# Attention and feed-forward block on eight cores: the projection groups of the next head are spread singly between the score matmuls instead of in pairs behind them

## The chip, the cores and the metric

The kernel runs on all eight cores of one Trainium2 chip. No core talks to another: each takes one half of the 2048 query rows of one of the four batch entries, and computes K and V for all 2048 rows of that entry itself. The metric is the device time of the slowest core in microseconds (us). The program before was run eight times: median 2807.35 us, lowest 2803.17, highest 3047.69. Six of the eight lie between 2803.17 and 2808.51 us, the other two at 2934.46 and 3047.69.

## The reference

```python
def attn(x, w_q, w_k, w_v, w_o):            # 16 heads of 128, D = 2048, S = 2048, B = 4
    q = (x @ w_q.T).reshape(B, S, H, Hd)    # k and v alike
    scores = einsum('bqhd,bkhd->bhqk', q, k) / sqrt(128)
    p = softmax(scores, axis=-1)
    o = einsum('bhqk,bkhd->bqhd', p, v).reshape(B, S, D)
    return o @ w_o.T
def ffn(x, w_gate, w_up, w_down):           # hidden 8192
    return (silu(x @ w_gate.T) * (x @ w_up.T)) @ w_down.T
x = x + layernorm(attn(layernorm(x), ...))
x = x + layernorm(ffn(layernorm(x), ...))
```

## The kernel before, in words

The kernel is written engine by engine: every operation is appended to the list of its engine in the order in which the Python text emits it, and each engine works through its own list in that order. Waits are explicit: an engine stops at a wait until a counter that another engine raises has reached a number. So the order of the text is the order of the work on each engine, and an instruction that waits holds back all that stands behind it on that engine.

The stages are: layer norm and transpose of the input; the query projection of all heads (L307); the attention stage; the output projection (L565) with the two layer norms around it; the gate and up projections (L653, L665); the down projection (L712); and the last layer norm with the residual. Only the attention stage is touched.

**The attention stage** loops over 16 heads. In this text a head has four rounds, r = 0 to 3, and each round handles four tiles of 128 keys:

- *Scores* S0 to S15 (`emit_scores_tc`, L426): two matmuls of 128x512 for a tile of 128 keys by 1024 queries, into one of two PSUM areas of two banks each, used in turn.
- *Exponentials* E0 to E15 (L435) on ScalarE: read one score area, write one of four slots of the tile PTR. E(n) of a round waits for its scores, for the value product of the round before (L448, counter tRd), because that product reads PTR, and for the sum of the round before on VectorE (counter vSm), which reads PTR too. S(n) waits for E(n-2), which frees the score area.
- *Value product* PV0 to PV3 (`emit_pv_round`, L448): eight matmuls that read the four PTR slots of one round. It is emitted one round late: PV(r-1) stands behind the first two score tiles of round r.
- *Sum* (`emit_tree_round`, L459 to L477): four VectorE additions per round for the softmax denominator.
- *Filler* (`emit_kv_group`, L354): the K and V projections of the **next** head, in eight groups K0 to K3 and V0 to V3 of 16 matmuls each, two groups per round. Each is accumulated in PSUM bank 4 or 5 and copied out by ScalarE (`emit_kv_evac`, L371). A group waits until the group two before it has been copied out. K0 and K1 wait also for the reciprocal of the head before (L525, counter vRc), since the reciprocal reads banks 4 and 5.

Behind the last round stand PV3, the transposes of V for the next head (L386, copied to SBUF by VectorE at L398), two matmuls with ones that sum the denominator over partitions (L517), then on VectorE the reciprocal (L525, its input in banks 4 and 5) and the scaling of the output (L529). The first two score tiles of a head wait for the two copies at L398. The last head has no next one and no filler.

The names used below: S, E, PV, K and V with a number as above; "evacuation" is the ScalarE copy at L371; "round 0" begins at S0.

Of the kernel before, what the change touches and what calls it, by code (L numbers as in the profile page):

```python
# [13 lines left out]
H = 16  # L14
# [63 lines left out]
def build_nc():  # L78
# [23 lines left out]
    def Bv(off, dims, parts=128):  # L102
        return bass.AP(ABF, off, [[ABF_N, parts]] + [list(d) for d in dims])

    def Fv(off, dims, parts=128):
        return bass.AP(AFP, off, [[AF32_N, parts]] + [list(d) for d in dims])

    def Pv(off, dims, parts=128):
        return bass.AP(PS, off, [[4096, parts]] + [list(d) for d in dims])
# [58 lines left out]
    def op(e, f, ride=None):  # L168
        pair = None
        if ride is not None:  # L170
            c, k = ride
            c.n += k
            pair = (c.s, k)
        if pair is None:
            ops[e].append(f)
        else:
            def g(eng, f=f, pair=pair):
                f(eng).then_inc(*pair)
            ops[e].append(g)

    def w(e, c, v=None):
        if v is None:
            c, v = c
        ops[e].append(lambda eng, s=c.s, v=v: eng.wait_ge(s, v))
# [149 lines left out]
    def emit_kv_group(kind, h, g):  # L334
        slot, dwv = wk_slot[h] if kind == "K" else wv_slot[h]
        if g == 0:
            w("t", dW[slot], dwv)
        if kind == "K":
            if h == 0:
                w("t", vA, 4 * (g + 1))  # L340
            if h == 0 and g < 2:
                w("t", sQe, 16)
            elif g < 2 and h >= 1:
                w("t", kv_evac[("V", h - 1, g + 2)])
            elif g >= 2:
                w("t", kv_evac[("K", h, g - 2)])
            if h >= 2 and g < 2:
                w("t", vRc, h - 1)
        else:
            w("t", kv_evac[("K", h, g + 2)] if g < 2 else kv_evac[("V", h, g - 2)])  # L350
        bank = 4 + (g % 2)
        for kc in range(NKC):
            ride = (tKV, 1) if kc == NKC - 1 else None
            op("t", lambda e, slot=slot, kc=kc, g=g, bank=bank: e.matmul(  # L354
                Pv(bank * 512, [(1, 512)]),
                Bv(W3 + slot * 2048 + kc * 128, [(1, 128)]),
                Bv(LN1 + kc * 2048 + g * 512, [(1, 512)]),
                start=(kc == 0), stop=(kc == NKC - 1)), ride)
        kv_mm[(kind, h, g)] = (tKV, tKV.n)
        if kind == "K" and g == 3:  # L360
            consumed_at[16 + 2 * h] = (tKV, tKV.n)
        if kind == "V" and g == 3:
            consumed_at[17 + 2 * h] = (tKV, tKV.n)

    def emit_kv_evac(kind, h, g):
        w("s", kv_mm[(kind, h, g)])
        if kind == "V" and g == 0 and h >= 1:
            w("s", vt_mm[(h - 1, 1)])
        bank = 4 + (g % 2)
        dst = (KSB + (h % 2) * 2048) if kind == "K" else VFM  # L370
        op("s", lambda e, g=g, dst=dst, bank=bank: e.activation(  # L371
            Bv(dst + g * 512, [(1, 512)]),
            Pv(bank * 512, [(1, 512)]), AF.Copy), (sKV, 1))
        kv_evac[(kind, h, g)] = (sKV, sKV.n)
# [38 lines left out]
    for h in range(H):  # L413

        def emit_scores_tc(tc, h=h):
            pair = tc % 2
            if tc == 0:
                w("t", kv_evac[("K", h, 3)])
                w("t", vVt, 2 * h + 1)
            elif tc == 1:  # L420
                w("t", vVt, 2 * h + 2)
            else:
                w("t", sE, 16 * h + tc - 1)
            for half in range(2):
                ride = (tS, 1) if half == 1 else None
                op("t", lambda e, tc=tc, half=half, pair=pair, h=h: e.matmul(  # L426
                    Pv(pair * 1024 + half * 512, [(1, 512)]),
                    Bv(KSB + (h % 2) * 2048 + tc * 128, [(1, 128)]),
                    Bv(QF + h * 1024 + half * 512, [(1, 512)]),
                    start=True, stop=True), ride)  # L430
            r = tc // 4
            w("s", tS, 16 * h + tc + 1)
            w("s", tRd, 4 * h + r)
            w("s", vsm, 4 * h + r)
            op("s", lambda e, tc=tc, pair=pair: e.activation(  # L435
                Bv(PTR + (tc % 4) * 1024, [(1, 1024)]),
                Pv(pair * 1024, [(1, 1024)]),
                AF.Exp, bias=Fv(ST + 41, [(1, 1)]), scale=QK), (sE, 1))

        def emit_pv_round(r, h=h):  # L440
            w("t", sE, 16 * h + 4 * (r + 1))
            if r == 0:
                w("t", vO, h)
            for i in range(4):
                tcv = 4 * r + i
                for half in range(2):
                    ride = (tRd, 1) if (i == 3 and half == 1) else None
                    op("t", lambda e, tcv=tcv, i=i, half=half, r=r: e.matmul(  # L448
                        Pv(3072 + half * 512, [(1, 512)]),
                        Bv(VTM + tcv * 128, [(1, 128)]),  # L450
                        Bv(PTR + i * 1024 + half * 512, [(1, 512)]),
                        start=(r == 0 and i == 0), stop=(r == 3 and i == 3)), ride)

        def emit_tree_round(r, h=h):
            w("v", sE, 16 * h + 4 * (r + 1))
            with_lp = "bf16 softmax denominator tree (rvr impact <1e-5)"
            def t1f(e):
                with nc.allow_low_precision(with_lp):
                    return e.tensor_tensor(Bv(WDA, [(1, 1024)]),  # L459
                                           Bv(PTR, [(1, 1024)]),  # L460
                                           Bv(PTR + 1024, [(1, 1024)]), ALU.add)
            def t2f(e):
                with nc.allow_low_precision(with_lp):
                    return e.tensor_tensor(Bv(WDA + 1024, [(1, 1024)]),
                                           Bv(PTR + 2048, [(1, 1024)]),
                                           Bv(PTR + 3072, [(1, 1024)]), ALU.add)
            def t3f(e):
                with nc.allow_low_precision(with_lp):
                    return e.tensor_tensor(Bv(WDA, [(1, 1024)]),
                                           Bv(WDA, [(1, 1024)]),  # L470
                                           Bv(WDA + 1024, [(1, 1024)]), ALU.add)
            def accf(e, r=r):
                with nc.allow_low_precision(with_lp):
                    if r == 0:
                        return e.tensor_copy(Bv(RB, [(1, 1024)]),
                                             Bv(WDA, [(1, 1024)]))
                    return e.tensor_tensor(Bv(RB, [(1, 1024)]),  # L477
                                           Bv(RB, [(1, 1024)]),
                                           Bv(WDA, [(1, 1024)]), ALU.add)
            op("v", t1f, (vI, 1))  # L480
            op("v", t2f, (vI, 1))
            w("v", vI, vI.n)
            op("v", t3f, (vI, 1))
            w("v", vI, vI.n)
            op("v", accf, (vsm, 1))

        for r in range(4):
            emit_scores_tc(4 * r)
            emit_scores_tc(4 * r + 1)
            if r >= 1:  # L490
                emit_pv_round(r - 1)
            emit_scores_tc(4 * r + 2)
            emit_scores_tc(4 * r + 3)
            if h + 1 < H:
                if r < 2:
                    emit_kv_group("K", h + 1, 2 * r)
                    emit_kv_evac("K", h + 1, 2 * r)
                    emit_kv_group("K", h + 1, 2 * r + 1)
                    emit_kv_evac("K", h + 1, 2 * r + 1)
                else:  # L500
                    emit_kv_group("V", h + 1, 2 * (r - 2))
                    emit_kv_evac("V", h + 1, 2 * (r - 2))
                    emit_kv_group("V", h + 1, 2 * (r - 2) + 1)
                    emit_kv_evac("V", h + 1, 2 * (r - 2) + 1)
            emit_tree_round(r)
        emit_pv_round(3)
        if h + 2 < H:
# [426 lines left out]
```

How the kernel before makes its waits and increments, by code:

```python
            def g(eng, f=f, pair=pair):  # L177
                f(eng).then_inc(*pair)
# [2 lines left out]
    def w(e, c, v=None):  # L181
        if v is None:
            c, v = c
        ops[e].append(lambda eng, s=c.s, v=v: eng.wait_ge(s, v))
```

## Time and profile before

| | before |
|---|---|
| median of 8 runs | 2807.35 us (2803.17 to 3047.69) |
| time of the profiled execution | 2803.17 us |
| its span, slowest core (core 1) | 2801.6 us |
| spans of the eight cores | 2790.1 to 2801.6 us |
| TensorE matmul busy | 2393.0 us, 85% |
| VectorE busy | 647.8 us, 23% |
| ScalarE busy | 590.1 us, 21% |
| L354, K and V projection | 513.5 us in 2048 matmuls |
| L426 / L448, scores / value product | 148.6 / 124.1 us in 512 matmuls each |
| L525, reciprocal | 104.8 us in 16 |

The span is the time between the first and the last instruction of one core; the time of an execution has 1.57 us more. "Idle before" is time in which the engine stood still just ahead of a group, with the instruction that ended most of it. The granted clock (PEclk) is the share of the full TensorE rate that the chip allowed in a stretch.

### The profile page before, as it was taken

The page shows a single profiled execution, that of the slowest core. Times are in us where ns is not written, and L with a number is a line of the kernel's source. Part 1 is how long each engine was busy: PE and PEld are TensorE (multiplying, and loading weights), DVE is VectorE, ACT ScalarE, POOL GpSimd, SP SyncE. Part 2 cuts the span into 40 slices and gives each one's busy share as a digit, 9 for nine tenths or more (in the row PEclk, how much of TensorE's full clock was granted, in tenths as well). Part 3 has the DMA queues.
Part 4 walks back from the last instruction along what each step waited for, and adds up shares of the span by engine and source line. Part 5 has one row for each costly group of instructions (what it writes and reads, how often), then busy time and mean ns, then how long its engine had stood idle before and what let it go on. Part 6 is the DMA issues. An engine that isn't in the chain of part 4 may idle for free.

```text
span 2801.6 us, 26992 instructions; the slowest of 8 cores (2790.1 to 2801.6 us)
## 1 busy us (share of the span) xinstructions
PE 2393.0 (85%) x10912; PEld 1059.9 (38%) x10912; DVE 647.8 (23%) x760; ACT 590.1 (21%) x677; POOL 157.7 (6%) x269
## 2 busy tenths in 40 slices
PE   1998788888788888687799999999999999999960
PEld 1443333333333333233444444444444444444420
DVE  5501433333433333465400100000000001010021
ACT  5513333333333333222000000000000001010021
POOL 0000000000000000000000000000000000111000
PEclk9999989998998998888899999999999999999985
DMA  6541100100100100723444444444444445545478
GB/s 189 137 89 23 23 16 15 23 16 15 23 16 16 23 15 1 120 90 105 76 75 76 75 77 78 78 77 76 75 76 76 82 61 75 75 69 77 73 123 155
DMA packets 67624, 186.35 MB, mean 67 GB/s; under 512 B 4912, under 2 KB 37680, under 8 KB 62256
## 3 DMA queue, kind: packets, MB, share of 16 engines
q0 software_dynamic: 64048, 159.47, 34.3%
q1 hardware_dynamic: 3456, 25.17, 3.0%
q8 instruction: 89, 1.46, 0.2%
q14 instruction: 31, 0.25, 0.0%
HBM read 302.12 MB, written 25.17 MB: 117 GB/s over the span
## 4 chain that ended last, share of the span: by engine, by line
PE 77%; DVE 9%; DMA 4%; issue 4%; ACT 3%; another core or an unknown queue 2%; ACTq 0%; DVEq 0%; POOL 0%; POOLq 0%
PE ps L354 18%; PE ps L653 16%; PE ps L665 16%; PE ps L712 15%; PE ps L307 4%; PE ps L448 4%; DVE afp L525 4%; PE ps L426 3%; ACT abf L435 2%; DMA x2s<-afp 2%; DVE afp L194 1%; DMA out<-afp 1%; DVE abf L398 1%; DVE afp L582 1%
## 5 line engine op out<-in xcount | busy, mean ns | idle before, releaser
L354 PE MATMUL ps<-abf 128*128 128x512 bf16 x2048 | 513.5, 415 | 54.7 <-DVE afp L525 53.4
L712 PE MATMUL ps<-abf 128*128 128x512 bf16 x2048 | 448.3, 382 | 16.0 <-DVE abf L736 8.6
L653 PE MATMUL ps<-abf 128*128 128x512 bf16 x2048 | 454.2, 380 | 2.6 <-DVE abf L633 2.6
L665 PE MATMUL ps<-abf 128*128 128x512 bf16 x2048 | 452.5, 379 | 0.0
L354 PEld LDWEIGHTS ps<-abf 128*128 128x128 bf16 x2048 | 214.9, 105 | 348.6 <-issue 147.9
L435 ACT ACTIVATE abf<-ps,afp 128x1024 bf16<-128x1024 f32 x256 | 270.5, 1111 | 166.8 <-PE ps L448 103.6
L712 PEld LDWEIGHTS ps<-abf 128*128 128x128 bf16 x2048 | 200.8, 98 | 263.5 <-issue 27.5
L653 PEld LDWEIGHTS ps<-abf 128*128 128x128 bf16 x2048 | 200.6, 98 | 245.6 <-issue 5.0
L665 PEld LDWEIGHTS ps<-abf 128*128 128x128 bf16 x2048 | 200.6, 98 | 241.4
L681 DVE TENSOR_TENSOR abf<-afp,ps 128x1024 bf16<-128x1024 f32 x64 | 78.2, 1222 | 809.2 <-PE ps L665 809.2
L426 PE MATMUL ps<-abf 128*128 128x512 bf16 x512 | 148.6, 386 | 124.9 <-ACT abf L435 105.8
L676 ACT ACTIVATE afp<-ps 128x1024 f32<-128x1024 f32 x64 | 65.5, 1023 | 804.4 <-PE ps L653 804.4
L371 ACT ACTIVATE abf<-ps 128x512 bf16<-128x512 f32 x128 | 76.4, 597 | 444.9 <-PE ps L354 444.9
L459 DVE TENSOR_TENSOR abf<-abf 128x1024 bf16<-128x1024 bf16 x64 | 44.1, 690 | 516.0 <-ACT abf L435 516.0
L565 PE MATMUL ps<-abf 128*128 128x512 bf16 x512 | 126.9, 415 | 31.7 <-DVE abf L605 23.4
L448 PE MATMUL ps<-abf 128*128 128x512 bf16 x512 | 124.1, 386 | 4.6 <-DVE abf L529 3.1
L426 PEld LDWEIGHTS ps<-abf 128*128 128x128 bf16 x512 | 38.9, 96 | 223.5 <-issue 202.3
L307 PE MATMUL ps<-abf 128*128 128x512 bf16 x512 | 114.9, 386 | 2.7 <-DVE abf L266 2.7
L736 DVE CAST abf<-ps 128x512 bf16<-128x512 f32 x16 | 9.9, 684 | 438.2 <-PE ps L712 438.2
L525 DVE RECIPROCAL afp<-ps 128x1024 f32<-128x1024 f32 x16 | 104.8, 6549 | 1.3 <-PE ps L517 1.3
L719 ACT ACTIVATE abf<-ps 128x512 bf16<-128x512 f32 x16 | 8.3, 604 | 444.3 <-PE ps L712 444.3
L565 PEld LDWEIGHTS ps<-abf 128*128 128x128 bf16 x512 | 53.2, 105 | 105.8 <-issue 55.8
(78 smaller groups left out, 976.6 us busy)
## 6 DMA issues: line engine op xcount, KB each, us to landing
abf<-wg POOLq DMA_DIRECT2D x64, 512.0 KB, 5.1
abf<-wu POOLq DMA_DIRECT2D x64, 512.0 KB, 5.1
abf<-wd POOLq DMA_DIRECT2D x64, 512.0 KB, 5.4
afp<-xb SPq DMA_DIRECT2D x24, 1024.0 KB, 7.1
abf<-wq POOLq DMA_DIRECT2D x16, 512.0 KB, 7.9
abf<-wk POOLq DMA_DIRECT2D x16, 512.0 KB, 5.2
abf<-wv POOLq DMA_DIRECT2D x16, 512.0 KB, 5.1
abf<-wo POOLq DMA_DIRECT2D x4, 2048.0 KB, 34.5
```

What stands on the lines that cost most here:

```text
L307: op("t", lambda e, slot=slot, kc=kc, half=half, pair=pair: e.matmul(Pv(2048 + pair * 1024 + half * 512, [(1, 512)]), Bv(W3 + slot * 2048 ...
L354: op("t", lambda e, slot=slot, kc=kc, g=g, bank=bank: e.matmul(Pv(bank * 512, [(1, 512)]), Bv(W3 + slot * 2048 + kc * 128, [(1, 128)]), Bv ...
L371: op("s", lambda e, g=g, dst=dst, bank=bank: e.activation(Bv(dst + g * 512, [(1, 512)]), Pv(bank * 512, [(1, 512)]), AF.Copy), (sKV, 1))
L426: op("t", lambda e, tc=tc, half=half, pair=pair, h=h: e.matmul(Pv(pair * 1024 + half * 512, [(1, 512)]), Bv(KSB + (h % 2) * 2048 + tc * 12 ...
L435: op("s", lambda e, tc=tc, pair=pair: e.activation(Bv(PTR + (tc % 4) * 1024, [(1, 1024)]), Pv(pair * 1024, [(1, 1024)]), AF.Exp, bias=Fv(S ...
L448: op("t", lambda e, tcv=tcv, i=i, half=half, r=r: e.matmul(Pv(3072 + half * 512, [(1, 512)]), Bv(VTM + tcv * 128, [(1, 128)]), Bv(PTR + i ...
L525: op("v", lambda e: e.reciprocal(Fv(T1, [(1, 1024)]), Pv(2048, [(1, 1024)])), (vRc, 1))
L565: op("t", lambda e, kc=kc, j=j, qc=qc, pair=pair: e.matmul(Pv(pair * 2048 + j * 512, [(1, 512)]), Bv(OFM + kc * 1024 + qc * 128, [(1, 128) ...
L653: op("t", lambda e, slot=slot_g, kc=kc, half=half, gb=gb: e.matmul(Pv(gb * 512 + half * 512, [(1, 512)]), Bv(W3 + slot * 2048 + kc * 128, ...
L665: op("t", lambda e, slot=slot_u, kc=kc, half=half, ub=ub: e.matmul(Pv(ub * 512 + half * 512, [(1, 512)]), Bv(W3 + slot * 2048 + kc * 128, ...
L681: op("v", lambda e, hc=hc, ub=ub: e.tensor_tensor(Bv(GMAP[hc], [(1, 1024)]), Fv(T1, [(1, 1024)]), Pv(ub * 512, [(1, 1024)]), ALU.mult), (v ...
L712: op("t", lambda e, hc=hc, qc=qc, i=i, base=base, j=j: e.matmul(Pv(qc * 512, [(1, 512)]), Bv(GMAP[hc] + qc * 128, [(1, 128)]), Bv(base + i ...
```

## The change

The two filler groups of a round no longer stand together behind its fourth score tile. The first stands behind the value product (in round 0 behind S1), ahead of the round's third score tile, and the second behind the fourth. Each evacuation moves with its group, so on ScalarE one evacuation now stands between the second and the third exponential of a round. The groups, their order among themselves and all their waits are the same.

```diff
+        def emit_filler(h, idx):
+            if h + 1 >= H:
+                return
+            kind = "K" if idx < 4 else "V"
+            emit_kv_group(kind, h + 1, idx % 4)
+            emit_kv_evac(kind, h + 1, idx % 4)
+
         for r in range(4):
             emit_scores_tc(4 * r)
             emit_scores_tc(4 * r + 1)
             if r >= 1:
                 emit_pv_round(r - 1)
+            emit_filler(h, 2 * r)
             emit_scores_tc(4 * r + 2)
             emit_scores_tc(4 * r + 3)
-            if h + 1 < H:
-                if r < 2:
-                    emit_kv_group("K", h + 1, 2 * r)
-                    emit_kv_evac("K", h + 1, 2 * r)
-                    emit_kv_group("K", h + 1, 2 * r + 1)
-                    emit_kv_evac("K", h + 1, 2 * r + 1)
-                else:
-                    emit_kv_group("V", h + 1, 2 * (r - 2))
-                    emit_kv_evac("V", h + 1, 2 * (r - 2))
-                    emit_kv_group("V", h + 1, 2 * (r - 2) + 1)
-                    emit_kv_evac("V", h + 1, 2 * (r - 2) + 1)
+            emit_filler(h, 2 * r + 1)
             emit_tree_round(r)
```

On TensorE, the start of head 1 (its round 0), with the counters that each instruction waits for. L517 is the sum with ones of head 0, L426 the scores, L354 the filler. Before:

```order
L517 MATMUL ps<-abf 128x512 [waits vSm,sKV]
L517 MATMUL ps<-abf 128x512
L426 MATMUL ps<-abf 128x512 [waits sKV,vVt]
L426 MATMUL ps<-abf 128x512
L426 MATMUL ps<-abf 128x512 [waits vVt]
L426 MATMUL ps<-abf 128x512
L426 MATMUL ps<-abf 128x512 [waits sE]
L426 MATMUL ps<-abf 128x512
L426 MATMUL ps<-abf 128x512 [waits sE]
L426 MATMUL ps<-abf 128x512
L354 MATMUL ps<-abf 128x512 [waits dW2,sKV,vRc]
L354 MATMUL ps<-abf 128x512 x15
```

The same place in the changed kernel, where the line of the sum with ones is L515:

```order
L515 MATMUL ps<-abf 128x512 [waits vSm,sKV]
L515 MATMUL ps<-abf 128x512
L426 MATMUL ps<-abf 128x512 [waits sKV,vVt]
L426 MATMUL ps<-abf 128x512
L426 MATMUL ps<-abf 128x512 [waits vVt]
L426 MATMUL ps<-abf 128x512
L354 MATMUL ps<-abf 128x512 [waits dW2,sKV,vRc]
L354 MATMUL ps<-abf 128x512 x15
L426 MATMUL ps<-abf 128x512 [waits sE]
L426 MATMUL ps<-abf 128x512
L426 MATMUL ps<-abf 128x512 [waits sE]
L426 MATMUL ps<-abf 128x512
```

K0, with its wait for vRc (the reciprocal of the head before), has moved ahead of S2 and S3, which now stand behind it.

On ScalarE, the first rounds of head 0. L435 is an exponential, L371 an evacuation; the first eight of L371 are those of head 0's own K and V. Before:

```order
L314 ACTIVATE abf<-ps 128x1024 x9
L371 ACTIVATE abf<-ps 128x512 x8
L435 ACTIVATE abf<-ps,afp 128x1024 x4
L371 ACTIVATE abf<-ps 128x512 x2
L435 ACTIVATE abf<-ps,afp 128x1024 x4
```

And in the changed kernel:

```order
L314 ACTIVATE abf<-ps 128x1024 x9
L371 ACTIVATE abf<-ps 128x512 x8
L435 ACTIVATE abf<-ps,afp 128x1024 x2
L371 ACTIVATE abf<-ps 128x512
L435 ACTIVATE abf<-ps,afp 128x1024 x2
L371 ACTIVATE abf<-ps 128x512
```

One evacuation of each round has moved ahead of the third exponential, which now stands behind it and so behind the filler group that it copies.

## Rows read from the trace of the kernel before

**Rows 1.** The page: span, and the chain that ended last, by line.
```profile
span 2801.6 us, 26992 instructions; the slowest of 8 cores (2790.1 to 2801.6 us)
...
PE ps L354 18%; PE ps L653 16%; PE ps L665 16%; PE ps L712 15%; PE ps L307 4%; PE ps L448 4%; DVE afp L525 4%; PE ps L426 3%; ACT abf L435 2%; DMA x2s<-afp 2%; DVE afp L194 1%; DMA out<-afp 1%; DVE abf L398 1%; DVE afp L582 1%
```

**Rows 2.** Groups by line, 282.19 to 1124.55 us; busy us, mean ns | idle before, releasers.
```profile
L354 PE MATMUL ps<-abf 128*128 128x512 bf16 x1792 | 453.0, 417 | 53.4 <-DVE afp L525 53.4
...
L426 PE MATMUL ps<-abf 128*128 128x512 bf16 x448 | 128.6, 384 | 106.2 <-ACT abf L435 89.3 <-DVE abf L398 16.9
```

**Rows 3.** Timeline, rounds 2 and 3 of one head; start, length, instruction [idle before <-releaser].
```profile
610.69 1.03 PE L426 MATMUL ps<-abf 128*128 128x512 bf16 x4
...
611.55 1.89 PE L448 MATMUL ps<-abf 128*128 128x512 bf16 x8
613.60 4.17 ACT L435 ACTIVATE abf<-ps,afp 128x1024 bf16<-128x1024 f32 x4 [2.05 <-PE ps L448]
...
614.85 0.59 PE L426 MATMUL ps<-abf 128*128 128x512 bf16 x2 [1.41 <-ACT abf L435]
...
615.86 0.59 PE L426 MATMUL ps<-abf 128*128 128x512 bf16 x2 [0.41 <-ACT abf L435]
...
616.29 7.07 PE L354 MATMUL ps<-abf 128*128 128x512 bf16 x32
617.87 0.69 DVE L459 TENSOR_TENSOR abf<-abf 128x1024 bf16<-128x1024 bf16 x1 [10.97 <-ACT abf L435]
...
620.05 0.60 ACT L371 ACTIVATE abf<-ps 128x512 bf16<-128x512 f32 x1 [2.28 <-PE ps L354]
620.07 0.69 DVE L477 TENSOR_TENSOR abf<-abf 128x1024 bf16<-128x1024 bf16 x1
...
623.19 1.03 PE L426 MATMUL ps<-abf 128*128 128x512 bf16 x4
```

**Rows 4.** Timeline, the end of that head and round 0 of the next.
```profile
640.00 0.59 PE L517 MATMUL ps<-abf 128*128 128x512 bf16 x2
...
642.16 6.55 DVE L525 RECIPROCAL afp<-ps 128x1024 f32<-128x1024 f32 x1
...
642.39 0.59 PE L426 MATMUL ps<-abf 128*128 128x512 bf16 x2 [0.54 <-DVE abf L398]
...
644.45 0.59 PE L426 MATMUL ps<-abf 128*128 128x512 bf16 x2 [0.54 <-ACT abf L435]
...
648.86 9.09 PE L354 MATMUL ps<-abf 128*128 128x512 bf16 x32 [3.82 <-DVE afp L525]
...
657.79 1.03 PE L426 MATMUL ps<-abf 128*128 128x512 bf16 x4
```

**Rows 5.** TensorE timeline: two ends of heads, and two fillers of round 0.
```profile
282.19 0.59 PE L517 MATMUL ps<-abf 128*128 128x512 bf16 x2
...
469.49 10.02 PE L354 MATMUL ps<-abf 128*128 128x512 bf16 x32 [3.82 <-DVE afp L525]
...
769.82 8.35 PE L354 MATMUL ps<-abf 128*128 128x512 bf16 x32 [3.81 <-DVE afp L525]
...
1124.55 0.59 PE L517 MATMUL ps<-abf 128*128 128x512 bf16 x2
```

**Rows 6.** Windows: stretch, busy of each engine (instructions), granted clock, DMA, GB/s.
```profile
610.80:623.30 12.50, 10.68 (x50) 4.55 (x48) 2.68 (x4) 5.37 (x6) 0.53 (x1) 1.00 0.24 42
623.30:637.40 14.10, 12.28 (x50) 4.91 (x48) 2.68 (x4) 5.37 (x6) 0.00 (x0) 0.88 0.00 1
...
1500.00:1800.00 300.00, 300.00 (x1392) 135.98 (x1391) 26.07 (x22) 22.51 (x22) 22.82 (x44) 1.00 0.46 77
```

**Rows 7.** TensorE timeline of head 0.
```profile
226.46 0.59 PE L426 MATMUL ps<-abf 128*128 128x512 bf16 x2 [0.54 <-DVE abf L398]
...
238.69 1.03 PE L426 MATMUL ps<-abf 128*128 128x512 bf16 x4
...
279.57 1.89 PE L448 MATMUL ps<-abf 128*128 128x512 bf16 x8
```

## The prediction, made before the changed kernel had run

> **What bounds the kernel now.** I read the chain of waits first. By line, L354, L448, L426 and the reciprocal at L525 hold 18, 4, 3 and 4% of it [rows 1], so the attention stage is near a third of the path, and TensorE sets its pace apart from the reciprocal. Then I read the groups by line over heads 1 to 14, which are the stretch between two of the L517 rows. It lasts 1124.55 - 282.19 = 842.36 us, 60.17 us a head [rows 5]. In it TensorE stood idle ahead of scores for 106.2 us, 89.3 of them released by exponentials, and ahead of the filler for 53.4 us, released by the reciprocal [rows 2].
>
> The timeline shows where in a round. A round from S to S lasts 623.19 - 610.69 = 12.50 us [rows 3]. Its 48 matmuls at the full rate take 48 x 0.216 = 10.37 us. (0.216 us is the pace of the four scores that start at 610.69 and end where the value product starts, at 611.55, [rows 3].) So 2.13 us of the round are gaps. They stand at two places: behind the value product S6 has to wait for E4 (1.41 us shown as idle), and S7 for E5 (0.41 us); the rest is the drain of a matmul, which the row counts as busy. E4 itself couldn't start earlier, for it overwrites what the value product reads, and it starts 2.05 us after that product starts [rows 3]. Thirty-two filler matmuls stand right behind S7, doing nothing for this gap.
>
> The clock comes next. The round of 12.50 us ran at a granted clock of 1.00, the next one took 14.10 us at 0.88 [rows 6]: part of it stood at the lower level, 1.2 GHz instead of 2.4. A filler pair that lasts 7.07 us [rows 3] takes 8.35 to 10.02 us behind the reciprocal wait [rows 5].
>
> **Part 1: the gaps of rounds 1 to 3.** The first filler group now stands between the value product and S6. It takes 16 x 0.216 = 3.46 us. Count from the start of a round. PV starts at 0.86 and ends at 2.59. E4 starts at 0.86 + 2.05 = 2.91. One exponential takes 1.11 us and the next starts 1.02 us after it (four in 4.17 us, [rows 3]), so E4 ends at 4.0, E5 at 5.0. The filler runs from 2.59 to 6.05 and S6 starts there, 2 us after E4 ended; S7 at 6.48, past E5. Both gaps go: 3 rounds x 14 heads x 2.13 = 89.5 us.
>
> What comes late next? ScalarE now has the evacuation ahead of E6. A reader of a finished matmul group starts 0.32 us after the full-rate end of the group (PV: 611.55 + 1.73 = 613.28, E4 at 613.60, [rows 3]). So the evacuation runs from 6.37 to 6.97 (0.60 us, [rows 3]), E6 from there to 8.1 and E7 to 9.1. The second filler covers 6.91 to 10.37. Next round's S8 needs E6 (2.2 us to spare), PV1 needs E7 and starts at 11.2 (2.1 us to spare). The sum on VectorE starts when E7 has ended, at 9.1, and takes 620.07 + 0.69 - 617.87 = 2.89 us [rows 3], to 12.0; E8, which needs it, could start at 10.37 + 2.91 = 13.3. That is the thinnest cover, 1.3 us. If it were gone, each microsecond past it would delay E8 by as much, and would show on TensorE only past the further 2 us by which the filler outlasts E4. At the end of a head the same sum, ready at 12.0, is wanted by the two matmuls with ones, behind PV3 and the transposes, at 10.37 + 2.62 = 13.0 (2.62 us from PV3 to L517: 282.19 - 279.57, [rows 5, 7]). VectorE is also due to copy V there, in the same order as before, from about 12.9. I put all of this at nothing.
>
> **Part 2: the clock in rounds 1 to 3.** The fillers of heads 1 to 14 took 453.0 us [rows 2], and 56 pairs at 7.07 us are 395.9, so 57.1 us are from the lower level. The fourteen pairs of round 0 have a mean of 9.02 us and lie between the two rows shown; (9.02 - 7.07) x 14 = 27.3 us of it are theirs. The remaining 29.8 us fell in rounds 1 to 3, behind gaps of 2.13 us. With the gaps gone TensorE has no reason to slow down there. Bounds: nothing gained (the clock falls for another reason), or 29.8 and a few more for scores that ran slow too. I take 29.8, since the windows put the clock at 1.00 wherever TensorE was busy without a break (1500 to 1800, [rows 6]).
>
> The Trainium skill, "TensorE: Matmul & The Clock Gate", section "HAM oscillation — how this bites in real kernels", lays the fall of the clock on a single long wait of the engine. By that rule the short gaps here would not explain it and the 29.8 us would stay: the result would be that of the second case below. Its section "A second HAM failure mode: psum-queue depth-cycling" says that many short idles between groups of matmuls are enough, which gives the sum as I make it. The trace sides with the second: the falls come in rounds whose only idles are the short ones, though not in each of them. The round of 14.10 us had 14.10 - 12.28 = 1.82 us of idle, as had its neighbour at 1.00 [rows 6].
>
> **Part 3: round 0 of heads 1 to 14.** K0 must wait for the reciprocal, which ends at 642.16 + 6.55 = 648.71; K0 starts at 648.86 [rows 4]. Nothing about that start changes: the reciprocal hangs on L517 and two copies. But S2 and S3 used to run in the shadow of this wait (S3 at 644.45, [rows 4]), and now they are queued behind K0, with E2, E3, the evacuation of K0 and the sum behind them on ScalarE and VectorE. Cost: four matmuls x 0.216 = 0.86 us a head, 12.1 us in all. At the lower level it would be 1.73 us a head; I take the first, because the pairs of round 0 lose 1.28 to 2.95 us, which is 6 to 14 slow matmuls, fewer than the 16 that now run ahead of S2. The idle time ahead of K0 grows by the same work taken out, to 648.86 - (642.39 + 0.43) = 6.0 us in one piece, and the clock is low at its end before and after; I leave the 1.95 us of loss behind it unchanged. Bounds: it vanishes (27 us less), or all 36 matmuls of round 0 run at the lower level (36 x 0.216 - 1.95 = 5.8 us a head, 81 us more); both are far from any row.
>
> Are E2 and E3 in time? From K0's start: K0 ends at 3.46 + 1.95 = 5.4, its evacuation at 6.3, S2 and S3 end at 6.3, E2 at 7.4, E3 at 8.4, the sum at 11.3. S4 starts at 5.4 + 0.86 + 3.46 = 9.7, PV0 at 10.6, E4 at 12.6. Covered by 1.3 us.
>
> **Part 4: head 0.** No reciprocal precedes it. S1 starts at 226.46 and S4 at 238.69, 12.23 us [rows 7]; with K0 right behind S1, S2 and S3 behind that, and K1, it is 0.43 + 3.46 + 0.86 + 3.46 = 8.21: 4.0 us less. From S4 to PV3 it took 279.57 - 238.69 = 40.88 us [rows 7]; three rounds of 10.37 are 31.1: 9.8 us less, falls of the clock included. Together 13.8 us. The last head has no filler and is as before; so are all other stages, and the weight transfers, whose queue no emission is moved past and which have most of a head to arrive.
>
> **The sum.** 89.5 + 29.8 - 12.1 + 13.8 = 121.0 us. As a second way: a head becomes 8.86 (L517 to K0, [rows 4]) + 9.72 (to S4) + 31.1 + 2.62 = 52.3 us, against 60.17; 14 x 7.9 + 13.8 = 124. The profiled execution took 2803.2 us, which gives 2682. It was the fastest of the eight, and the undisturbed ones reach 2808.5, so a typical run of the changed kernel should lie 2 to 4 us above: 2685 us.
>
> **The rivals.**
>
> *The clock falls in rounds 1 to 3 all the same.* Its cause would be the reciprocal wait or the load of the chip. For it: falls come in most heads. Against: in the rows they follow gaps. Then 29.8 us, and some 3 in head 0, are not gained: 2718 us.
>
> *More is gained.* Round 0's slow matmuls become fewer because the clock's state is not pulled down again: up to 27 us, half of it 2671 us.
>
> *The waits come back on the other side (slower).* The place is ScalarE's queue: the evacuation holds E6 behind the filler, and E6, E7 and the sum end later than S8 and PV1 want them. The point from which it decides is 2.1 us of extra lateness a round at PV1. If it did, each round would carry its old 2.13 us again at S8 or PV1, the clock's falls would stay, and S2 and S3 would have lost their shadow: 2806 + 12 to 24 (at either level) = 2818 to 2830 us. Against it: the ends worked out above.
>
> *A denser stage is throttled (slower).* All eight cores would do matmuls without a break in a round, and the chip would cap the clock for the whole stage. A head has 192 x 0.216 = 41.5 us of matmuls. At a granted clock of 0.88, that of the slower round [rows 6], they would take 5.7 us more, 85 us in 15 heads: 2770 us. The whole gain of 121 us, 8.1 us a head, is used up at 41.5 / 49.6 = 0.84, and below that the kernel is slower: at 0.80 by 35 us, 2841 us. Against: from 1500 to 1800 us TensorE is 100% busy at a granted clock of 1.00 [rows 6]. The Trainium skill, same page, section "Seeing it yourself", states a cap at 13/16 (0.81) for three or more cores of a die with dense matmuls, by which the result would be about 2829 us; the trace of this case does not show it.
>
> **How the numbers follow.** The forecast 0.76, its own range 2674 to 2700; the clock's falls stay 0.10 (2718); more is gained 0.06 (2671); the waits come back 0.03 (2824); the cap 0.03 (2841); something between, as a sum on VectorE that isn't covered, 0.02 (2740). The range of 8 in 10 is 2670 to 2718. About 0.2%, 5.6 us, is what a measurement of this kernel can tell from no change. Faster 0.94; same 0.01; slower 0.05.
>
> **What would show it.** Each step has its row in the profile after. Part 1: no idle at L426 released by L435 in rounds 1 to 3, rounds of 10.4 us, so that "idle before" of L426 falls from 106.2 to about 20 (the V copies, [rows 2]). Part 2: filler groups of 16 in rounds 1 to 3 all at 3.5 to 3.6 us, and a granted clock of 1.00 there. Part 3: idle ahead of K0 from 3.82 to some 6 us, S4 about 18.6 us after L517 instead of 17.8, L517 to L517 52.4 us. I would be wrong if S8, PV1 or E8 shows a new wait of a microsecond (the third rival), if slow matmuls turn up in rounds without gaps (the first or fourth), or if K0 and K1 of round 0 together take much over 9 us.

## The result and the profile after

The changed kernel has a median of 2705.69 us in 11 executions (2682.09 to 3131.55), the kernel before 2808.17 us in 32 (2801.53 to 3226.37). Both medians hold executions in which some cores had a lower granted clock; over the others the ratio is 0.9591, 95% interval [0.9571, 0.9611]: 4.1% faster. Five of the eleven lie between 2682 and 2688 us. The forecast was 2685 us. The profiled execution took 2688.22 us.

The page of the changed kernel, its span and its chain by line, to be read beside [rows 1]; the lines below L354 count two less than before:

```profile
span 2686.7 us, 26781 instructions; the slowest of 8 cores (2668.6 to 2686.7 us)
...
PE ps L354 18%; PE ps L651 17%; PE ps L663 16%; PE ps L710 16%; PE ps L448 4%; PE ps L307 4%; DVE afp L523 4%; PE ps L426 4%; DMA x2s<-afp 2%; DVE afp L194 1%; DMA out<-afp 1%; DVE abf L398 1%; DVE afp L580 1%; DVE afp L588 1%
```

The exponential at L435, 2% of the chain before, is gone from it. The groups by line over heads 1 to 14, 268.38 to 1001.41 us (busy, mean of one | idle before), answer to [rows 2]:

```profile
L354 PE MATMUL ps<-abf 128*128 128x512 bf16 x1771 | 429.9, 398 | 83.5 <-DVE afp L523 82.2 <-issue 0.2
L426 PE MATMUL ps<-abf 128*128 128x512 bf16 x446 | 116.9, 379 | 17.2 <-DVE abf L398 17.1
```

The 89.3 us that scores spent waiting for exponentials are zero; the wait of the filler for the reciprocal has grown from 53.4 to 82.2. (Some matmul records are missing, 1771 for 1792, so busy times are a little low, and a row whose first record is missing starts 0.22 us late.) The timeline of one round, in all engines, answers to [rows 3]:

```profile
602.92 3.62 PE L354 MATMUL ps<-abf 128*128 128x512 bf16 x16
603.24 2.12 ACT L435 ACTIVATE abf<-ps,afp 128x1024 bf16<-128x1024 f32 x2 [2.05 <-PE ps L448]
606.38 1.03 PE L426 MATMUL ps<-abf 128*128 128x512 bf16 x4
606.64 0.60 ACT L371 ACTIVATE abf<-ps 128x512 bf16<-128x512 f32 x1 [1.28 <-PE ps L354]
607.18 2.12 ACT L435 ACTIVATE abf<-ps,afp 128x1024 bf16<-128x1024 f32 x2
607.24 3.62 PE L354 MATMUL ps<-abf 128*128 128x512 bf16 x16
...
611.56 1.89 PE L448 MATMUL ps<-abf 128*128 128x512 bf16 x7
611.60 0.69 DVE L477 TENSOR_TENSOR abf<-abf 128x1024 bf16<-128x1024 bf16 x1
613.28 3.62 PE L354 MATMUL ps<-abf 128*128 128x512 bf16 x16
613.60 2.12 ACT L435 ACTIVATE abf<-ps,afp 128x1024 bf16<-128x1024 f32 x2 [2.05 <-PE ps L448]
...
616.74 1.03 PE L426 MATMUL ps<-abf 128*128 128x512 bf16 x4
```

The two exponentials that start at 603.24 lie wholly under the filler of 602.92. No TensorE row carries an idle time. From the scores at 606.38 to those at 616.74 is one round, 10.36 us for 12.50 before. The sum at L477 ends at 612.29, and the exponential that needs it starts at 613.60, held by the value product and not by the sum: the thin cover of 1.3 us holds as worked out. Round 0 answers to [rows 4]:

```profile
584.50 6.55 DVE L523 RECIPROCAL afp<-ps 128x1024 f32<-128x1024 f32 x1
584.73 0.59 PE L426 MATMUL ps<-abf 128*128 128x512 bf16 x2 [0.54 <-DVE abf L398]
591.16 1.23 DVE L527 TENSOR_TENSOR abf<-ps,afp 128x1024 bf16<-128x1024 f32 x1
591.20 4.98 PE L354 MATMUL ps<-abf 128*128 128x512 bf16 x16 [5.87 <-DVE afp L523]
596.02 1.03 PE L426 MATMUL ps<-abf 128*128 128x512 bf16 x4
```

S2 and S3 stand behind K0 now, and the idle time ahead of K0 is 5.87 us for 3.82. K0 takes 4.98 us where 16 matmuls at the full rate take 3.62. Over the 14 heads K0 takes 4.95 to 6.43 us, in the mean 5.63. The ends of heads, the sums with ones, answer to [rows 5]:

```profile
268.38 0.59 PE L515 MATMUL ps<-abf 128*128 128x512 bf16 x2
...
1001.41 0.38 PE L515 MATMUL ps<-abf 128*128 128x512 bf16 x1
```

Fourteen heads last 733.03 us, 52.36 each (the last row lacks one of its two matmuls, so the true figure is 0.22 us lower for all fourteen); before 842.36, 60.17 each. And the granted clock of one round, to be read beside [rows 6]:

```profile
606.38:616.74 10.36, 10.31 (x49) 4.71 (x49) 2.68 (x4) 5.38 (x6) 0.53 (x1) 1.00 0.32 52
```

### The profile page after: what moved, and what is told of

Same layout as the page of the kernel before. It is cut to its first block, busy times and chain, and to the rows that moved or that the text cites. A ratio compares the mean times of both kernels' runs of the same rounds, so it can differ in the third digit from the quotient of the medians.

```text
span 2686.7 us, 26781 instructions; the slowest of 8 cores (2668.6 to 2686.7 us)
## 1 busy us (share of the span) xinstructions
PE 2337.5 (87%) x10701; PEld 1060.3 (39%) x10912; DVE 649.0 (24%) x760; ACT 588.4 (22%) x677; POOL 158.3 (6%) x269
## 4 chain that ended last, share of the span: by engine, by line
PE 80%; DVE 10%; DMA 4%; issue 2%; another core or an unknown queue 2%; ACT 1%; DVEq 0%; POOL 0%; ACTq 0%; POOLq 0%
PE ps L354 18%; PE ps L651 17%; PE ps L663 16%; PE ps L710 16%; PE ps L448 4%; PE ps L307 4%; DVE afp L523 4%; PE ps L426 4%; DMA x2s<-afp 2%; DVE afp L194 1%; DMA out<-afp 1%; DVE abf L398 1%; DVE afp L580 1%; DVE afp L588 1%
## 5 line engine op out<-in xcount | busy, mean ns | idle before, releaser
L354 PE MATMUL ps<-abf 128*128 128x512 bf16 x2020 | 486.2, 395 | 85.1 <-DVE afp L523 82.2
L710 PE MATMUL ps<-abf 128*128 128x512 bf16 x2007 | 447.7, 383 | 18.2 <-DVE abf L734 8.6
L651 PE MATMUL ps<-abf 128*128 128x512 bf16 x2007 | 454.7, 382 | 5.6 <-DVE abf L631 3.5
L663 PE MATMUL ps<-abf 128*128 128x512 bf16 x2007 | 452.6, 381 | 2.2
L354 PEld LDWEIGHTS ps<-abf 128*128 128x128 bf16 x2048 | 205.9, 101 | 350.2 <-issue 128.8
L435 ACT ACTIVATE abf<-ps,afp 128x1024 bf16<-128x1024 f32 x256 | 272.7, 1111 | 166.6 <-PE ps L448 108.7
L426 PE MATMUL ps<-abf 128*128 128x512 bf16 x510 | 137.2, 384 | 27.1 <-DVE abf L398 19.3
L563 PE MATMUL ps<-abf 128*128 128x512 bf16 x502 | 131.5, 428 | 28.8 <-DVE abf L603 19.7
L371 ACT ACTIVATE abf<-ps 128x512 bf16<-128x512 f32 x128 | 76.4, 597 | 325.9 <-PE ps L354 325.9
L448 PE MATMUL ps<-abf 128*128 128x512 bf16 x489 | 123.8, 389 | 5.8 <-DVE abf L527 3.1
L307 PE MATMUL ps<-abf 128*128 128x512 bf16 x499 | 112.7, 383 | 3.7 <-DVE abf L266 3.0
L523 DVE RECIPROCAL afp<-ps 128x1024 f32<-128x1024 f32 x16 | 104.8, 6549 | 0.9 <-PE ps L515 0.9
L426 PEld LDWEIGHTS ps<-abf 128*128 128x128 bf16 x512 | 47.0, 98 | 99.8 <-issue 50.3
```

Source lines behind the costliest of these rows:

```text
L307: op("t", lambda e, slot=slot, kc=kc, half=half, pair=pair: e.matmul(Pv(2048 + pair * 1024 + half * 512, [(1, 512)]), Bv(W3 + slot * 2048 ...
L371: op("s", lambda e, g=g, dst=dst, bank=bank: e.activation(Bv(dst + g * 512, [(1, 512)]), Pv(bank * 512, [(1, 512)]), AF.Copy), (sKV, 1))
L435: op("s", lambda e, tc=tc, pair=pair: e.activation(Bv(PTR + (tc % 4) * 1024, [(1, 1024)]), Pv(pair * 1024, [(1, 1024)]), AF.Exp, bias=Fv(S ...
L448: op("t", lambda e, tcv=tcv, i=i, half=half, r=r: e.matmul(Pv(3072 + half * 512, [(1, 512)]), Bv(VTM + tcv * 128, [(1, 128)]), Bv(PTR + i ...
L523: op("v", lambda e: e.reciprocal(Fv(T1, [(1, 1024)]), Pv(2048, [(1, 1024)])), (vRc, 1))
L563: op("t", lambda e, kc=kc, j=j, qc=qc, pair=pair: e.matmul(Pv(pair * 2048 + j * 512, [(1, 512)]), Bv(OFM + kc * 1024 + qc * 128, [(1, 128) ...
```

## The experiments

My theory: the gain is the covering of E4 and E5 by the first filler of a round, with the falls of the clock that the gaps had caused; the new order of round 0 is a loss. Against it stood, above all, that a wait comes back elsewhere, and that the clock falls whatever the order is. The kernel before ran in the same hour as each experiment: 2806.57 us median for the first four, 2808.84 for the next two. Diffs are against the changed kernel.

**Round 0 in its old order.**

```diff
-            emit_filler(h, 2 * r)
+            if r >= 1:
+                emit_filler(h, 2 * r)
             emit_scores_tc(4 * r + 2)
             emit_scores_tc(4 * r + 3)
+            if r == 0:
+                emit_filler(h, 0)
```

> The fillers are spread in rounds 1 to 3 as in the changed kernel, but round 0 keeps the order of before: S2 and S3 ahead of K0 and K1. My theory (S2 and S3 lost the shadow of the reciprocal, 0.86 us in each of heads 1 to 14, while head 0 gained 4.0 us): 12 us faster than the changed kernel from heads 1 to 14 and 4 slower from head 0, so 2676 to 2680 us where the changed kernel is near 2685; L515 to L515 51.5 us instead of 52.4. Rival (round 0's new order costs nothing, since its slow clock pays it back, or its second gap of idle time is what costs): the same time as the changed kernel or up to 10 us more.

Measured 2673.25 us (2670.98 to 2673.42), ratio 0.9525 [0.9512, 0.9539], so better than the changed kernel, whose interval doesn't touch it, and 3 us below the range that I expected. The timeline of TensorE, round 0 of one head and the two sums with ones around it:

```profile
580.83 0.59 PE L518 MATMUL ps<-abf 128*128 128x512 bf16 x2
...
584.15 0.59 PE L426 MATMUL ps<-abf 128*128 128x512 bf16 x2 [0.34 <-ACT abf L435]
585.28 0.59 PE L426 MATMUL ps<-abf 128*128 128x512 bf16 x2 [0.54 <-ACT abf L435]
589.68 8.75 PE L354 MATMUL ps<-abf 128*128 128x512 bf16 x32 [3.81 <-DVE afp L526]
...
631.97 0.59 PE L518 MATMUL ps<-abf 128*128 128x512 bf16 x2
```

Fourteen heads last 990.39 - 274.14 = 716.25 us, 51.16 each, 1.20 less than in the changed kernel. Of this 0.86 is S2 and S3 back in the shadow. The rest is clock: the pair of round 0 takes 8.75 us in most heads, 1.68 over 7.07, while K0 of the changed kernel is 2.0 us over 3.62 in the mean of its 14. Head 0 ends 274.14 - 268.38 = 5.8 us later. Of that, 4.0 are its round 0 (13.36 us from S0 to S4 for 9.33), as counted, and 1.7 lie before S0 (227.08 for 225.35 us), where the two kernels are the same. Net 14 x 1.20 - 5.8 = 11 us. Over all eight cores of each profile a head takes 51.12 to 51.35 us here and 52.26 to 52.41 in the changed kernel. The theory stands; its price for round 0, against this kernel, was 0.3 us a head too low on this core.

**Only round 0 in the new order.**

```diff
-            emit_filler(h, 2 * r)
+            if r == 0:
+                emit_filler(h, 0)
             emit_scores_tc(4 * r + 2)
             emit_scores_tc(4 * r + 3)
+            if r >= 1:
+                emit_filler(h, 2 * r)
```

> The reverse: the new order in round 0 alone, rounds 1 to 3 with both filler groups behind the fourth score tile, as before. Theory: the gaps of 2.13 us and the falls of the clock in rounds 1 to 3 are all back; round 0 costs 14 x 0.86 = 12 us and head 0 gives back 4: 8 us slower than before, 2810 to 2816 us where before is near 2805. Rival (round 0's order contributes to the gain): at or below 2800 us.

Measured 2806.57 us, ratio 1.0002 [0.9993, 1.0012]: no change, and below what I expected. The sums with ones, from the TensorE timeline (core 0):

```profile
275.37 0.59 PE L518 MATMUL ps<-abf 128*128 128x512 bf16 x2
...
1127.99 0.59 PE L518 MATMUL ps<-abf 128*128 128x512 bf16 x2
```

Heads 1 to 14 take 60.90 us each for 60.17, 0.73 more, 10.3 us in all. Round 0 itself costs about what I had priced at 0.86: from K0 to S4 it takes 9.82 us in the mean for 8.86, so 0.96 more; rounds 1 to 3 give 0.23 back. Head 0 ends 6.8 us earlier than before (282.19, [rows 5]), where I had counted 4.0: its round 0 gives these 4.0, a start of S0 1.1 us earlier on this core and one fall of the clock less give the rest. What I had not counted is that the falls in rounds 1 to 3 become fewer. On this core 17 of the 42 filler pairs are slow for 19 before; on the other seven it is 8 to 13, for 19 to 22 in the kernel before, and their heads take 59.67 to 60.48 us (60.13 to 60.40 before). Why a new order in round 0 changes the falls in the later rounds, no run shows. The new order of round 0 by itself has no part in the gain: what head 0 and the clock win, round 0 of the later heads loses.

**Both fillers ahead of the third score tile.**

```diff
             emit_filler(h, 2 * r)
+            if r >= 1:
+                emit_filler(h, 2 * r + 1)
             emit_scores_tc(4 * r + 2)
             emit_scores_tc(4 * r + 3)
-            emit_filler(h, 2 * r + 1)
+            if r == 0:
+                emit_filler(h, 1)
```

> In rounds 1 to 3 both filler groups stand between the value product and the third score tile, none behind the fourth. This makes the slower rival of the prediction happen: E6 waits behind two evacuations and ends at about 11.5 us from the round's start, E7 at 12.5, where S8 and PV1 want them at 10.4 and 11.2. Theory (where a score's exponential is covered decides, not that a filler stands ahead of S6): idle at S8, S9 and PV of about 2.0 us a round, 45 rounds, and falls of the clock as before: 2795 to 2815 us. Rival (what matters is only that the value product is followed by filler): within 20 us of the changed kernel, 2685 to 2705 us.

Measured 2775.13 us, ratio 0.9884 [0.9865, 0.9903]. The timeline, from the last part of a filler to the last value product of a head:

```profile
537.37 0.60 ACT L371 ACTIVATE abf<-ps 128x512 bf16<-128x512 f32 x1 [2.86 <-PE ps L354]
...
537.91 2.12 ACT L435 ACTIVATE abf<-ps,afp 128x1024 bf16<-128x1024 f32 x2
539.17 0.59 PE L426 MATMUL ps<-abf 128*128 128x512 bf16 x2 [1.03 <-ACT abf L435]
...
540.18 0.59 PE L426 MATMUL ps<-abf 128*128 128x512 bf16 x2 [0.41 <-ACT abf L435]
...
542.33 7.07 PE L354 MATMUL ps<-abf 128*128 128x512 bf16 x32
...
564.43 1.89 PE L448 MATMUL ps<-abf 128*128 128x512 bf16 x8 [2.04 <-ACT abf L435]
```

The wait is back on the other side, at S8 and S9 (1.03 and 0.41 us), and at PV3 (2.04 us), by the mechanism that the prediction named: E6 stands behind two evacuations and ends at 537.91 + 1.11 = 539.02 us, where S8 wants it at 537.97, when S7 has left TensorE. From the filler at 530.20 to that at 542.33 a round is 12.13 us, a gap of 1.76. A head takes 58.46 us for 52.36 in the changed kernel, 2.03 a round. So what is worth most is not filler behind the value product as such, but filler at both places where an exponential is awaited. I had expected 2795 to 2815 us because I added the falls of the clock; with gaps of 2.0 us in 45 rounds and no falls it would have been 2685 + 90 = 2775, which it is. Indeed none of its filler pairs of rounds 1 to 3 is longer than 7.07 us, on any core, 28 of which follow such a gap, where before 19 of 42 were longer, by 1.2 to 1.7 us. This run moves the gap and makes it smaller at once, so it doesn't say which of the two stopped the falls.

**Four matmuls of filler ahead, twelve behind.** The filler helper takes a range of its 16 matmuls; the evacuation follows the last of them.

```diff
-            emit_filler(h, 2 * r)
+            emit_filler(h, 2 * r, 0, 4 if r >= 1 else NKC)
             emit_scores_tc(4 * r + 2)
             emit_scores_tc(4 * r + 3)
+            if r >= 1:
+                emit_filler(h, 2 * r, 4, NKC)
             emit_filler(h, 2 * r + 1)
```

> In rounds 1 to 3 only four of the sixteen matmuls of the first filler group stand ahead of the third score tile, the other twelve behind the fourth. They cover 0.86 us of the gap of 2.13 us, so 1.27 us stay in each of 45 rounds, 57 us. If the clock falls behind gaps only of some length, none is left in rounds 1 to 3: about 2742 us, 0.5 us of idle at S6 and 0.4 at S7. If it falls with every gap: the 33 us of before come on top, about 2775 us.

Measured 2745.13 us, ratio 0.9783 [0.9767, 0.9799], 3 us from the first number. TensorE, one round (L430 is the scores, L356 the filler, L452 the value product there):

```profile
305.39 1.03 PE L356 MATMUL ps<-abf 128*128 128x512 bf16 x4
306.97 0.59 PE L430 MATMUL ps<-abf 128*128 128x512 bf16 x2 [0.55 <-ACT abf L439]
307.97 0.59 PE L430 MATMUL ps<-abf 128*128 128x512 bf16 x2 [0.41 <-ACT abf L439]
308.40 6.21 PE L356 MATMUL ps<-abf 128*128 128x512 bf16 x27
314.44 1.03 PE L430 MATMUL ps<-abf 128*128 128x512 bf16 x4
```

The cover works by the microsecond: 0.86 us of filler took 0.86 us off the idle time at S6 (1.41 to 0.55) and nothing off S7. The 28 matmuls behind take 6.20 or 6.21 us in all 42 rounds of heads 1 to 14, the full rate. Here the gaps stand where they stood before, behind the value product, and only their size has changed. Of the 121 us, then, the gaps are the larger part and the falls of the clock the smaller, and the falls vanish before the gaps do.

**The reciprocal reads a copy.** What is left of idle time in a head hangs on K0's wait for the reciprocal, which holds banks 4 and 5. Here ScalarE copies them to SBUF first.

```diff
             if h >= 2 and g < 2:
-                w("t", vRc, h - 1)
+                w("t", sRB, h - 1)
...
-        w("v", tRB, h + 1)
+        w("s", tRB, h + 1)
+        if h >= 1:
+            w("s", vRc, h)
+        op("s", lambda e: e.activation(
+            Fv(T1 + 1024, [(1, 1024)]),
+            Pv(2048, [(1, 1024)]), AF.Copy), (sRB, 1))
+        w("v", sRB, h + 1)
...
-            Fv(T1, [(1, 1024)]), Pv(2048, [(1, 1024)])), (vRc, 1))
+            Fv(T1, [(1, 1024)]), Fv(T1 + 1024, [(1, 1024)])), (vRc, 1))
```

> The changed kernel, and ScalarE copies the partition sums of the denominator from PSUM banks 4 and 5 to SBUF (one copy of 128x1024); the reciprocal reads the copy, and K0 and K1 wait for the copy instead of the reciprocal. Theory (the reciprocal wait of 5.9 us is all that is left of idle time in a head, and its clock loss of about 2 us hangs on it): K0 follows S1 at 2.8 us from L515 instead of 8.9, the reciprocal ends at 8.8 and is wanted by PV0 at 11.5; a head of 44.3 us instead of 52.4, 14 heads: 113 us faster than the changed kernel, 2565 to 2580 us. Rival (the reciprocal itself, or the sum of round 0 queued behind it on VectorE, becomes the bound): a wait at PV0 or E4 of several us a head, 2600 to 2680 us.

Measured 2573.91 us, ratio 0.9165 [0.9151, 0.9178], as the theory said. This is the best version: 8.4% under the kernel before. The timeline of round 0 (L523 is the copy, L529 the reciprocal):

```profile
490.57 0.59 PE L515 MATMUL ps<-abf 128*128 128x512 bf16 x2
491.32 1.02 ACT L523 ACTIVATE afp<-ps 128x1024 f32<-128x1024 f32 x1 [2.51 <-PE ps L515]
...
492.74 6.54 DVE L529 RECIPROCAL afp<-afp 128x1024 f32<-128x1024 f32 x1
492.97 0.59 PE L426 MATMUL ps<-abf 128*128 128x512 bf16 x2 [0.54 <-DVE abf L398]
493.40 3.62 PE L354 MATMUL ps<-abf 128*128 128x512 bf16 x16
```

K0 follows S1 without a gap, and the reciprocal, as long as ever, lies beside it. No value product waits, so the rival doesn't show. A head is 44.29 us. The window of heads 1 to 14 has TensorE busy for 603.23 of 620.12 us at a granted clock of 1.00:

```profile
269.12:889.24 620.12, 603.23 (x2944) 276.25 (x2941) 285.54 (x281) 316.26 (x350) 15.09 (x28) 1.00 0.14 23
```

**The same copy with the old filler order.** The diff is the one above, on the kernel before.

> The same copy with the filler order of before. Theory: the reciprocal wait (3.8 us shown, 4.0 with its drain) and its clock loss of 1.95 us go, 6 us a head; the gaps of rounds 1 to 3 and their falls of the clock stay: 84 us faster than before, 2715 to 2730 us. S2 and S3 now stand in the open, so the new order and the copy should together give more than the sum of both alone (121 + 84 = 205 us; with e5 at 2573 it is 232 us). Rival (the two gains overlap): e5 is less than 205 us faster than before.

Measured 2721.24 us, ratio 0.9695 [0.9681, 0.9709]. The copy alone brings 3.05%, the new order alone 4.09%, both together 8.35%: about 86 and 115 us apart (122 by the changed kernel's times near 2684 us), 234 us together, at 2806 us. They help each other by 2.1 us a head. With the reciprocal's wait, the old order hides S2 and S3 under it and the new one pays 0.9 us for them. Without it, the old order has them in the open, with their own waits for exponentials: K0 starts 4.88 us after the sums with ones (502.28 - 497.40), for 2.83 in the kernel with both changes. The TensorE timeline of that head:

```profile
497.40 0.59 PE L515 MATMUL ps<-abf 128*128 128x512 bf16 x2
...
502.28 7.07 PE L354 MATMUL ps<-abf 128*128 128x512 bf16 x32
...
525.86 0.59 PE L426 MATMUL ps<-abf 128*128 128x512 bf16 x2 [1.41 <-ACT abf L435]
...
527.41 8.63 PE L354 MATMUL ps<-abf 128*128 128x512 bf16 x32
```

The falls of the clock also stay where the gaps stay: its heads last between 51.92 us and 55.57 us, and 19 of its 42 filler pairs of rounds 1 to 3 are slow, as before (13 to 19 over its eight cores, 19 to 22 before). This answers the first rival of the prediction where it lays the falls on the reciprocal's wait. The wait is gone here, no idle time of TensorE in heads 1 to 14 is longer than 1.69 us, and the pair of round 0 takes 7.07 us in every head, yet the falls are there.

**Half of PV3 behind the sums with ones.** The kernel with the copy, whose last idle time is the wait for the copies of V.

```diff
-        emit_pv_round(3)
+        emit_pv_round(3, 0, 2 if h + 1 < H else 4)
...
+        if h + 1 < H:
+            emit_pv_round(3, 2, 4)
         w("s", tRB, h + 1)
```

> The kernel with the copy and the spread fillers, and of PV3 only the first four matmuls stay ahead of the transposes; the other four stand behind the two matmuls with ones, in the wait for the copies of V. Theory (at the end of a head TensorE waits only for those copies, 0.67 and 0.54 us shown, 1.5 us with the drains): the transposes and so the copies come 0.86 us earlier and the four matmuls fill idle time: 15 heads x 0.86 = 13 us less, 2558 to 2564 us, L515 to L515 43.4 us. Rival (the sum of the last round on VectorE, ready at 12.0 us from the round's start, now holds the copies, due at 12.0): 2565 to 2575 us.

Measured 2597.95 us (2596.92 to 3039.39), ratio 0.9137 [0.9098, 0.9176]; the kernel before took 2849.51 us in that hour and 2806 to 2809 in the others, so the ratio says little and I compare with the kernel with the copy: 24 us more than its 2573.91, and 46.05 us a head for 44.29; heads 1 to 14 alone are 644.65 - 620.12 = 24.5 us longer. Both theories fail, and the timeline shows why (L449 is the value product, L516 the sum with ones):

```profile
312.53 0.59 PE L516 MATMUL ps<-abf 128*128 128x512 bf16 x2
312.96 1.02 PE L449 MATMUL ps<-abf 128*128 128x512 bf16 x4
...
314.09 2.35 DVE L398 CAST abf<-ps 128x1024 bf16<-128x1024 f32 x2 [1.81 <-PE ps L449]
315.46 0.59 PE L426 MATMUL ps<-abf 128*128 128x512 bf16 x2 [1.48 <-DVE abf L398]
...
317.14 5.18 PE L354 MATMUL ps<-abf 128*128 128x512 bf16 x16
```

The copy of the next head's V (L398) overwrites what PV3 reads, so it waits for the counter tRd, which the last matmul of PV3 raises; it is released by L449 and not by the transposes. I had moved that matmul behind, and with it the copy on which the next head waits. S0 comes 2.93 us after L516, for 1.27 in the kernel with the copy; and in every second head the clock falls with the longer gap (5.18 to 5.30 us for K0, 3.62 in the others).

## Why the prediction was right

*Part 1, the gaps.* Predicted 42 x 2.13 = 89.5 us, measured 42 x (12.50 - 10.36) = 89.9. All 42 rounds of heads 1 to 14 last 10.36 us. No wait took their place; the experiment with both fillers ahead shows where it would have come, at S8 behind E6 in ScalarE's queue.

*Part 2, the clock.* Predicted 29.8 us. Rounds 1 to 3 of the 14 heads, from S4 to PV3, took 557.6 us before and take 435.1 after, 122.5 less; the gaps are 89.9 of it, so the clock gave 32.6. The 2.8 above the forecast are scores that had run slow too, which the prediction mentions and puts at nothing. No filler of 16 in rounds 1 to 3 is longer than 3.62 us after. The falls went with gaps of 2.13 us a round, and by the experiment with the copy and the old order they need no long wait beside them. So the section "HAM oscillation — how this bites in real kernels" of the Trainium skill ("TensorE: Matmul & The Clock Gate"), which lays the fall on one long wait, doesn't account for them, and the section "A second HAM failure mode: psum-queue depth-cycling", which lays it on many short idles, does.

*Part 3, round 0.* The mechanism was right and the term nearly: from K0 to S4 round 0 takes 137.0 us over the 14 heads for 124.0 before, 0.93 a head where 0.86 was predicted. I left the clock loss behind the reciprocal unchanged at 1.95 us, and it is 2.0. The 1.20 us of the first experiment is against a kernel whose pairs of round 0 lose 1.7 us on that core, and 1.65 to 1.9 in the mean of each of its cores; that part of the clock's loss the prediction didn't have, and why it is smaller there stays open.

*Part 4, head 0.* Predicted 13.8 us less; it ends at 268.38 instead of 282.19, 13.8 less, and both steps are as worked out (S0 to S4 9.33 us for 13.36, S4 to PV3 31.1 for 40.9). That it fits to 0.1 us is partly luck. Before, head 0 lasted 52.70 to 56.86 us from S0 to the sums with ones, by the falls that a core happened to have, and the core of [rows 7] had the most; after, it lasts 43.03 on all eight. So the cores gained 9.7 to 13.8.

*The sum.* Heads 1 to 14 became 109.3 us shorter. The first way of the sum had 107.2 for them (89.5 + 29.8 - 12.1), the second 110. With head 0 that is 123 us up to the last head, predicted 121 and 124. The profiled execution shows 115 us less, because from the start of head 15 on it took 1685.3 us on its slowest core for 1677.1 before. The prediction put this at nothing ("the last head has no filler and is as before"). Of these 8.2 us, 2.2 are head 15, 38.15 us for 35.98; over the eight cores it takes 37.0 to 38.4 for 35.6 to 36.0. The other 6.0 lie behind it, on core 2, which had a lower granted clock there (below). They are not shown to come from it: in the kernel with the copy core 1 took as long behind head 15, 1647 us, without it. The median of all eleven executions, 2705.69 us, is inside the range of 8 in 10 and outside the forecast's own 2674 to 2700.

*The rivals.* The clock's falls did not stay (2718 us). More was not gained (2671 us): K0 loses 2.0 us. The waits did not come back. When they were forced, with both fillers ahead, they cost 2.03 us a round, near the 2.13 of the prediction, but the falls did not stay with them, so its 2818 to 2830 us was too high: 2775.13. No cap on the clock appears in the attention stage of the profiled execution; it does in the repeat below, at 0.81, where a head of core 4 takes 60.29 us and the gain of the order is used up, as the prediction worked out for a clock below 0.84.

## What to carry to other kernels

Independent work in the queue of a busy engine is worth most in front of the instruction that will wait, in a piece just longer than the wait; in one block behind it, it covers nothing. Count the moved block's own waits too: here its first piece waits for a reciprocal, so whatever is moved behind that piece leaves a shadow that was free, and as long as that wait stands the best order differs between the first round and the others. When an order pays less than it could, look for the buffer that couples it to a slow engine: a copy of 1.02 us that freed two PSUM banks from a reciprocal of 6.5 us gave some 110 us on top of the 122 of the reordering. And before an instruction is moved behind another, look for who waits for it: the half of PV3 that was to fill idle time held up the copy for which the next head waits.

## What the runs showed of the hardware

*Short gaps can halve the clock, and shorter ones here did not.* With 2.13 us of gaps a round, 19 of 42 filler pairs ran partly at the lower level (1.2 GHz for 2.4), with the reciprocal's wait in the kernel and without it. None of the 28 behind gaps of 1.76 us did, and none of the 42 blocks behind gaps of 1.27 us.

*A third level of the granted clock.* In the profiled execution of the changed kernel cores 2 and 3 were lower for a while in the output projection, between 1110 and 1272 us. The same 20 us of core 2 and of core 1:

```profile
1130.00:1150.00 20.00, 18.22 (x69) 7.48 (x70) 11.92 (x13) 4.56 (x6) 0.53 (x1) 0.81 0.35 113
```

```profile
1130.00:1150.00 20.00, 16.55 (x77) 7.36 (x76) 11.88 (x14) 4.56 (x6) 0.53 (x1) 1.00 0.34 106
```

The 0.81 is not a mean of full and half rate: the clock records of the trace hold 0.8125 as a value of its own, for 127 us on core 2, 124 on core 3 and none on the other six. I ran the changed kernel once more to see whether this comes with its denser attention stage:

> The changed kernel once more, unaltered. Its first eleven times hold four between 2705 and 2729 us, in which a pair of cores has a granted clock of 0.92 to 0.93, beside five at 2682 to 2688; the spread orders of the other experiments showed none of it. Theory (a disturbance of that hour or chip, not of the order): all fast times within 2680 to 2690 us, median 2684. Rival (the denser attention stage brings a mild cap on the clock with it): again about one time in three at 2700 to 2730 us.

It took 2798.88 us in the median (2787.45 to 3098.53) and the kernel before 2849.51 us on the same chip in the same hour, where it is at 2806 otherwise. So neither came, the 2680 to 2690 us of the theory or the one time in three of the rival: all eight were lower on some cores. Where a core kept its clock the order gave the same as ever: in five of the eight cores 0 to 3 have spans of 2670 to 2683 us. In its profile core 4 stood at 0.81 in the middle of a head, with TensorE busy 41.86 of 43 us:

```profile
288.00:331.00 43.00, 41.86 (x171) 17.40 (x168) 11.43 (x15) 17.30 (x19) 1.06 (x2) 0.81 0.14 25
```

Cores 4 and 5 were at this level for 806 and 803 us in all, cores 6 and 7 for 422 and 429, cores 0 to 3 never. The kernel with half of PV3 moved, profiled in the same hour, had it on all four cores 4 to 7 at once, for 119 to 127 us each between 1021 and 1182 us.

0.81 is what the Trainium skill, "TensorE: Matmul & The Clock Gate", section "Seeing it yourself", states as 13/16 for dense matmuls on three or more cores of a die. The trace of the kernel with half of PV3 moved agrees, with four cores of one die at 0.8125; the other two show it on a pair, with the other pair of the die at full rate for all or part of the time. Seven of the ten profiles of this case have it on no core, among them the densest: in the kernel with the copy TensorE is busy for 97% of the stretch from 269 to 880 us at a granted clock of 1.00 on every core. In that hour the kernel before too had pairs of cores with a mean clock near 0.91 for 0.94, but it has no profile of it. Whether the denser order makes the level more likely stays open.
